# One batch pair instead of two single batches: K's folded products of batches 0 and 1 in one round of 128 columns

## The reference

```
x = x + xattn(layernorm(x), ctx)     # q = ln(x) Wq, k = ctx Wk, v = ctx Wv, 8 heads of 64,
                                     # softmax(q k^T / 8) v, times Wo, plus bo
x = x + ffn(layernorm(x))            # bitlinear: activations rounded to 8 bits a token,
                                     # weights to -1, 0, 1; down(silu(gate(x)) * up(x))
```

## Time and profile before

| | |
|---|---|
| median of the three runs | 1103.5 us |
| the profiled execution's own time | 1102.12 us |
| its span, first to last instruction | 1100.3 us |
| TensorE busy | 1071.3 us, 97% |
| VectorE busy | 965.9 us, 88% |
| ScalarE busy | 743.9 us, 68% |
| GpSimd busy | 499.6 us, 45% |
| mean granted TensorE clock | 0.998 of 2.4 GHz |

### The profile page before, as it was taken

One profiled execution on the slowest core, in us unless ns is written; L12 is line 12 of the kernel. 1 busy time (PEld: TensorE's weight loads), 2 busy tenths in 40 slices (PEclk: granted clock), 3 DMA queues, 4 the chain that ended last, 5 costly groups with the idle time before them and its releaser, 6 DMA issues.

```text
span 1100.3 us, 17415 instructions
## 1 busy us (share of the span) xinstructions
PE 1071.3 (97%) x5466; PEld 493.7 (45%) x5528; DVE 965.9 (88%) x2085; ACT 743.9 (68%) x947; POOL 499.6 (45%) x641
## 2 busy tenths in 40 slices
...
GB/s 351 305 223 167 125 113 111 81 126 93 101 120 114 123 103 90 118 109 89 119 120 112 100 106 109 98 105 120 102 110 106 119 115 98 106 115 92 78 72 100
DMA packets 355963, 133.80 MB, mean 122 GB/s; under 512 B 332448, under 2 KB 332960, under 8 KB 355360
## 3 DMA queue, kind: packets, MB, share of 16 engines
...
...
## 4 chain that ended last, share of the span: by engine, by line
PE 78%; DVE 10%; ACT 4%; issue 3%; DMA 2%; SPq 1%; POOL 1%; ACTq 0%; DVEq 0%; POOLq 0%
PE ps L1383 34%; PE ps L1402 17%; PE ps L1319 8%; PE ps L1322 8%; PE ps L1320 8%; DMA FF<-FF 2%; DVE FF L1057 1%; DVE hm L1066 1%; PE ps L1312 1%; DVE bns L1043 1%; PE ps L1219 1%; DVE hm L1061 1%; PE ps L1307 1%; SPq L557 1%; PE ps L1250 1%
## 5 line engine op out<-in xcount | busy, mean ns | idle before, releaser
L1383 PE MATMUL ps<-wgT,FF 128*128 128x512 bf16 x1024 | 263.1, 379 | 1.3 <-DMA FF<-FF 0.9
L1383 PE MATMUL ps<-wW,FF 128*128 128x512 bf16 x1024 | 262.8, 379 | 0.4 <-DVE FF L1057 0.3
L1402 PE MATMUL ps<-wW,FF 128*128 128x512 bf16 x962 | 218.9, 379 | 7.0 <-DMA FF<-FF 3.8
L1057 DVE TENSOR_TENSOR FF<-FF,ps 128x512 f32<-128x512 f32 x256 | 173.8, 681 | 48.7 <-ACT FF L834 27.9
L834 ACT ACTIVATE FF<-ps,sgu 128x512 f32<-128x512 f32 x256 | 173.7, 682 | 60.8 <-PE ps L1383 58.7
L843 ACT ACTIVATE FF<-FF,c 128x1024 int16<-128x1024 f32 x128 | 141.4, 1143 | 74.3 <-DVE c L1070 73.7
L692 POOL TENSOR_TENSOR AT<-AT,rd 128x512 f32<-128x512 f32 x64 | 67.7, 1058 | 219.6 <-DVE rd L1102 215.9
L1402 PEld LDWEIGHTS ps<-wW,FF 128*128 128x128 bf16 x1024 | 99.5, 98 | 126.1 <-issue 7.5
L1383 PEld LDWEIGHTS ps<-wW,FF 128*128 128x128 bf16 x1024 | 99.7, 98 | 122.2 <-DVE FF L1057 3.3
L1383 PEld LDWEIGHTS ps<-wgT,FF 128*128 128x128 bf16 x1024 | 97.6, 98 | 123.8 <-issue 5.0
L680 POOL TENSOR_TENSOR xhl<-xn,xhl 128x512 f16<-128x512 f32 x64 | 74.5, 1164 | 82.5 <-ACT xhl L850 82.5
...
## 6 DMA issues: line engine op xcount, KB each, us to landing
...
```

The lines of the kernel that those rows point to most:

```text
L1057: eng.tensor_tensor(hh, hh, U[n % 2][:, :], ALU.mult).then_inc(v_h, 1)
L1383: mm = eng.matmul(bank[n % 2][:, :].rearrange("p (o f) -> p o f", o=4), qxT[:, i % 2, k, :], w[:, 4 * f:4 * f + 4, k, :], start=(k == 0), ...
L1402: mm = eng.matmul(y_bank(i)[:, :], hT[:, i % 2, c, :], wdT[:, c, :], start=(c == 0), stop=(c == 15))
```

## The change

K's product of batch 1 is no longer made by four rounds of its own. The four rounds of the opening (`first_X`, r < 4) take the columns of both batches, 128 instead of 64, into the two banks that `pair_of` gives. `hi` and `lo` read batch 0's half as before. New on ACT, `k_wide r` copies batch 1's half, scaled, as two pieces of 128x256 into slot 7 + r of x (f32), and `k_hi r` later makes the high part from there; new on POOL, `k_lo r` makes the low part. `load_x` of tiles 7 to 10 now waits for the `k_lo` that frees its slot. `b_wide`, `b_hi` and `b_lo` are left for V's four rounds. PE's `first_X` 2, 3, 6 and 7, the two transposes `max_turn 2` and `max_turn 3`, and `scores 0` wait for `k_wide` too. All five written orders are new, and the runs of `keep`.

```diff
-        KEEP = [('i', 16), ('i', 1), ('i', 1), ('i', 16), ('t', 9), ('t', 15), ('v', 2), ('v', 57), ('u', 7)]
+        KEEP = [('i', 16), ('i', 1), ('i', 2), ('i', 1), ('t', 38), ('t', 14), ('t', 12), ('t', 4), ('v', 55), ('u', 8), ('u', 36)]
...
+        def wide_k(r):
+            return xr[:, 7 + r, :]
...
-                "turn_p 1, turn_x 4, turn_w 1 1, turn_p 2, turn_x 5, turn_w 1 2, turn_q 0, turn_w 1 3, turn_x 6, "
+                "turn_p 1, turn_w 1 1, turn_x 4, turn_p 2, turn_w 1 3, turn_x 5, turn_q 0, turn_w 1 2, turn_p 3, "
...
-                    eng.wait_ge(v_cl[0][1], 1)
+                    eng.wait_ge(g_kl, t - 6)
...
+            def k_lo(r):
+                eng.wait_ge(a_kh, r + 1)
+                eng.tensor_tensor(chunk(1, 1, r), wide_k(r), chunk(1, 0, r), ALU.subtract).then_inc(g_kl, 1)
...
+            def k_wide(r):
+                eng.wait_ge(p_X, r + 1)
+                eng.wait_ge(v_lo, 2 * r + 2)
+                if r == 0:
+                    eng.wait_ge(v_cl[0][1], 1)
+                for z in range(2):
+                    eng.activation(wide_k(r).rearrange("p (q z l) -> p q z l", q=4, z=2)[:, :, 1 - z, :],
+                                   job_in(1, r)[:, z], ACT.Copy, scale=fwd[:, 0, 1:2]).then_inc(a_kw, 1)
+
+            def k_hi(r):
+                eng.wait_ge(a_kw, 2 * r + 2)
+                if r == 0:
+                    eng.wait_ge(v_cl[1][1], 1)
+                eng.activation(chunk(1, 0, r), wide_k(r), ACT.Copy).then_inc(a_kh, 1)
...
                 elif e >= 2:
                     eng.wait_ge(v_lo, 6)
+                    eng.wait_ge(a_kw, 6)
...
-                                o = 512 * ((z + b) % 2) + 64 * q
-                                mm = eng.matmul(pair_of(n)[:, o:o + 64],
-                                                wqT[h0, x, q, r * P:(r + 1) * P], split[0][h0, q, y, b * LC:(b + 1) * LC],
+                                o = 512 * z + P * q
+                                mm = eng.matmul(pair_of(n)[:, o:o + P],
+                                                wqT[h0, x, q, r * P:(r + 1) * P], split[0][h0, q, y, 0:2 * LC],
                                                 start=(x + y == 0), stop=(x == 1))
...
             def scores(j):
                 b = j // TPB
                 eng.wait_ge(t_x[j % 2], 16 * (j // 2 + 1))
+                if j == 0:
+                    eng.wait_ge(a_kw, 6)
...
-            for r in range(4):
-                put(jit_at(1, r) + 6.46, round_X, 1, r)
```

More of the change, by code:

```diff
@@ L200, in xattn_ffn @@
         g_jl = sem("g_jl")
+        a_kw = sem("a_kw")
+        a_kh = sem("a_kh")
+        g_kl = sem("g_kl")
         a_bw = sem("a_bw")
@@ L276, in queue, with jit_at @@
             return put, run
-        def jit_at(b, r):
-            return at(turn_of(r) // 4, turn_of(r) % 4 * .25 - .3)
-        def turn_of(r):
-            return (r + 4) % 8
+        def jit_at(r):
+            return at(r // 4, r % 4 * .25 - .3)
         def job_step(b, r):
@@ L362, in pair_of @@
         def pair_of(n):
-            o = 2048 if n < 8 and n % 2 == 0 else 3072
+            o = 2048 if n % 2 == 0 else 3072
             return banks[:, o:o + 1024]
@@ L700, in p_lo @@
                 eng.tensor_tensor(phl[:, 1, :], E[:, j % 2, :], phl[:, 0, :], ALU.subtract).then_inc(g_pl, 1)
+            def k_lo(r):
+                eng.wait_ge(a_kh, r + 1)
+                eng.tensor_tensor(chunk(1, 1, r), wide_k(r), chunk(1, 0, r), ALU.subtract).then_inc(g_kl, 1)
             def b_lo(r):
-                eng.wait_ge(a_bh, turn_of(r) + 1)
-                eng.tensor_tensor(chunk(1, 2 * (r // 4) + 1, r % 4), wide_j, chunk(1, 2 * (r // 4), r % 4),
-                                  ALU.subtract).then_inc(g_bl, 1)
+                eng.wait_ge(a_bh, r - 3)
+                eng.tensor_tensor(chunk(1, 3, r - 4), wide_j, chunk(1, 2, r - 4), ALU.subtract).then_inc(g_bl, 1)
             def j_lo(b, r, d):
@@ L714, in _ @@
             put(0.0, constants)
-            for r in range(8):
-                put(jit_at(1, r) + 7.99, b_lo, r)
+            for r in range(4):
+                put(jit_at(r) + 7.99, b_lo, r + 4)
+                put(jit_at(r + 4) + 7.99, k_lo, r)
             for b, r in JOBS:
@@ L771, in hi @@
                                scale=fwd[:, r // 4, b:b + 1]).then_inc(a_hi, 1)
+            def k_wide(r):
[11 more added lines that the diff above has]
+                eng.activation(chunk(1, 0, r), wide_k(r), ACT.Copy).then_inc(a_kh, 1)
             def b_wide(r):
-                eng.wait_ge(p_X, r + 1 if r >= 4 else 9 + r)
+                eng.wait_ge(p_X, r + 1)
                 if r == 4:
@@ L777, in b_wide @@
                 else:
-                    eng.wait_ge(g_bl, turn_of(r))
-                eng.activation(job_out(wide_j, r), job_in(1, r), ACT.Copy,
-                               scale=fwd[:, r // 4, 1:2]).then_inc(a_bw, 1)
+                    eng.wait_ge(g_bl, r - 4)
+                eng.activation(wide_j, job_in(1, r), ACT.Copy, scale=fwd[:, 1, 1:2]).then_inc(a_bw, 1)
             def b_hi(r):
-                eng.wait_ge(a_bw, turn_of(r) + 1)
-                if r == 0:
-                    eng.wait_ge(v_cl[1][1], 1)
-                eng.activation(chunk(1, 2 * (r // 4), r % 4), wide_j, ACT.Copy).then_inc(a_bh, 1)
+                eng.wait_ge(a_bw, r - 3)
+                eng.activation(chunk(1, 2, r - 4), wide_j, ACT.Copy).then_inc(a_bh, 1)
             def j_wide(b, r, d):
@@ L885, in _ @@
                 put(TERN_T[m][c], tern, m, c)
-            for r in range(8):
-                put(jit_at(1, r) + 7.1, b_wide, r)
-                put(jit_at(1, r) + 7.2, b_hi, r)
+            for r in range(4):
+                put(RNDV_T[r] + .2, k_wide, r)
+                put(jit_at(r) + 7.1, b_wide, r + 4)
+                put(jit_at(r) + 7.2, b_hi, r + 4)
+                put(jit_at(r + 4) + 7.2, k_hi, r)
             for b, r in JOBS:
@@ L1253, in keep, with first_X @@
                         eng.matmul(bank[:, 0:256], wqT[:, 0, 0, 0:P], wqT[:, 0, 0, 0:256], start=True, stop=True)
-            def round_X(b, r):
-                n = 8 * b + r
+            def first_X(r):
+                n = r
                 if n == 0:
@@ L1266, in round_X @@
                     eng.wait_ge(v_lo, 2 * n - 2)
+                    eng.wait_ge(a_kw, 2 * n - 2)
                 if n in (4, 6):
@@ L1297, in pair_X @@
                 if n == 0:
-                    eng.wait_ge(a_bw, 8)
+                    eng.wait_ge(a_bw, 4)
                 else:
@@ L1410, in _ @@
             for r in range(8):
-                put(RND_T[r], round_X, 0, r)
+                put(RND_T[r], first_X, r)
             for n in range(len(KEEP)):
```

16 lines of the change are left out of this document (7 added, 9 removed), and 232 rows, old and new, of the table OPENING.

## The result

The changed kernel takes 1106.22 us (median of 20 runs, 1103.77 to 1109.54) against 1102.97 us before (20 runs, 1100.32 to 1106.75), a ratio of the means of 1.0027 with the 95% interval 1.0016 to 1.0038. So the change costs about 3 us. That is less than the 0.5% at which this text calls two kernels different, but the interval leaves out 1, and the forecast (-1.7 us) has the wrong sign; the time itself, 1106.2 us, is still inside the range that was given. Two more measurements of the same kernel later gave 1.0023 (1.0008 to 1.0037) and 1.0016 (1.0003 to 1.0030).

A forecast was written before the change was run, and what follows sets the result against it. It took ACT, DVE and the DMA queue to bound the opening, and PE's work the rest. -2.25 + 1.75 + 0 - 1.2 = -1.7 us gave 1101.8 us, range 1096.5 to 1107.5.

The forecast's parts named there:

- Step 1: PE behind the first `gate_up`: four late rounds removed, 0.56 us each, all on the path; -2.25 us.
- Rival C: Up to 313 us DVE sets the pace, PE's 2.25 us return as waits: 0 to +2, 1104.5 us, chance 0.17.
- Step 6: PE's idle time up to 313 us, 3.2 us before: -1.2 us, bounds -3.2 to +3.
- Steps 3 and 4: Opening: ACT's added work, +3.0 us (bounds +0.6 to +4.3); through `turn_x 5`, `gate_up 0 0` then starts at 95.2, +1.8.
- Step 5: Third `gate_up` at 103.9 instead of 102.75: +1.2 us, or +1.75 with the removed round put apart; `silu 0 0` stays.
- Step 2: PE in the opening: four rounds widened to 128 columns add 1.4 us, covered by idle time, so counted as nothing.
- Step 8: 77 more `keep` matmuls, 8.6 us, in the opening where PE waits; no term, little to gain from the clock.
- Step 7: `load_x` 7 to 10 now wait for POOL's `k_lo`; nothing behind waits more than 1.2 us, counted as nothing.
- Rival B: Opening: w_down lands too late, `load_down` 2 and 3 being behind `turn_w 1 0`: +5.4, 1108.9 us, chance 0.13.
- Rival A: Opening comes out ahead, `gate_up 0 0` 1.7 us earlier, all 3.2 us of idle found: -7.1, 1096.4 us, chance 0.18.

The follow-up runs named there:

- g_four: Changed kernel with 96 matmuls of 64 columns, read by nothing, put back on PE in four groups near the late rounds' places: 1104.91 us, 1.0005 of before.
- h_without: Kernel before with its four late rounds left out on PE and nothing else changed: 1105.46 us, 1.0015 of before.
- k_light: Kernel before with three quarters of DVE's largest-value search left out for 14 tiles, 22 us less: 0.9970 of before.

## Why the prediction was wrong

- **Step 1 (PE's work removed, -2.25 us) is the step that failed.** "PE is full there, so this work lies on the path." The size was right: in g_four the next `gate_up` starts 0.46 us after a group, and with the switch a group puts 0.55 us between two of them. The conclusion was not. Removed alone from before, the rounds gave +0.0015 instead of -0.0020 (h_without); put back into the changed kernel they cost nothing (g_four, 1.0005). In the four pairs with and without them the stretch is 232.4 and 233.2 (two of before) against 234.5, 233.0 against 235.2 (mean of three), 230.3 against 230.6, and 230.7 against 230.3 us; the last pair alone has the sign that I gave to all. A busy share of 98% says that PE seldom waits now. It does not say that PE would still not wait if it got there sooner.
- **Rival C was the right mechanism**, PE's gain not passed on, and my argument against it the error: "PE's idle is only 3.2 us, so DVE cannot have ended many waits." Waits that PE's own work just covers are in no list. DVE's work was worth 3.3 us in before all the same, about 2 of them at equal clock (k_light). The Trainium skill, page "Perfetto Trace Analysis", section "Identifying the Most-Contended Engine", says to improve the engine with the highest occupancy first, and to judge TensorE by MFU (the share of its peak arithmetic) and by the busy share of its weight loads, not by its matmul time. By weight loads that points to VectorE here (88% against PEld's 45%); I went by matmul time, 98%, and MFU was not worked out. The runs side with VectorE: 2.25 us less on PE gave nothing, 22 us less on DVE gave 3.3 us.
- **Step 6 (idle time -1.2 us) failed with it.** Named waits behind the first `gate_up` went from 2.5 and 3.2 us to 4.2, 7.0 and 6.6. The one wait that I wanted to see go did shrink, from 1.2 us (2.2 in the second profile of before) to 0.2; `gate_up`'s waits for `silu`, `mult` and turns took its place.
- **Steps 3 and 4 had the right sign and were too small.** I took +3.0 at the end of `abs_sum 2 3` (81.5 before); it came at 87.0, and at 85.2 in the second profile. `gate_up 0 0` came 2.5 us late in the mean of the profiles, not 1.8. The amount of ACT's work was right: 4.3 us up to the end of `abs_sum 2 3` and 1.1 behind it are 5.4 forecast, and 5.2 more were busy ahead of `tern 2 0`. The covers that I set against it were not there: ACT's idle time ahead of `tern 2 0` fell by 0.7 us in the mean of the profiles. And `turn_x 4` behind the late `turn_p 1` was a second chain that I had not looked at: I counted only the order behind `turn_x 5`.
- **Step 5**: the third `gate_up` came at 106.1, 104.4 and 105.1 us against 103.9 forecast, close in one profile of three. `silu 0 0` does pace it, and my sentence that it stays was wrong: `turn_w 2 0`, on which it hangs, went at 98.45 us in the first profile and 96.84 in the second, instead of 96.24.
- **Step 2 held.** The wide rounds run at 32 ns a matmul (1.51 us for 48). The 81 ns a pair of the Trainium skill (page "TensorE: Matmul & The Clock Gate", section "Back-to-back issue gap") are not what this stream does.
- **Step 8 (`keep`, no term) was set at too little.** I wrote that of the clock "little is to be had there". The granted clock of the opening went from 0.98 to 1.00, and executions of before differ by 5.5 us between clocks of 1.000 and 0.993 to 0.995. That is worth 2 to 3 us in the ratios, in favour of the change; at equal clock the forecast is off by 6.6 us and not by 4 to 5.
- **Step 7 (the slots, 0) held, and only by the order.** `load_x 7` did not wait in the changed kernel; moving one `k_lo` past one `p_norm` made it wait 11.1 us.
- **Rival B did not happen**: `load_down 2` and `3` were issued at 71.92 us, at the early end of the 71 to 76 that it reckoned with, and `abs_sum 2 2` did not wait for them. **Rival A** is refuted by `gate_up 0 0` itself.

In sum: steps 1 and 6 together were to shorten the stretch by 3.45 us; it grew by 0.7 us from the first profile of before to the first of now, by 2.4 in the means. `gate_up 0 0` was to come 1.8 us late and came 2.5. By the means that is 4.9 us, as the spans have it and the timed executions at equal clock; 2 to 3 us in the ratio, since before is often granted less clock. That the result lies only 4 us from the forecast is thus in part luck: the clock made up for a part of what steps 1, 3, 4 and 6 had wrong. Open is why the kernel before does not gain from having its rounds removed even with DVE relieved, why the added waits of the changed kernel vary from 4.2 to 7.0 us between profiles, and why it is, with four groups, if anything faster than without (1.0005 against 1.0016 to 1.0027). No version that computes everything was faster than the kernel before.
